# Value rows of a causal attention: unpadded through memory, spread into the padded tile on GpSimd

## The reference

```
xn = layernorm(x)
Q, K, V = (xn @ W.T) split into 16 heads of 16, for W_q, W_k, W_v
scores = Q K^T * 16**-0.5, masked with the lower triangle
s = (softmax(scores) @ V) joined @ W_o.T
```

## Time and profile before

| what | us |
| --- | --- |
| three runs | 2177.48, 2183.09, 2172.04 |
| median | 2177.48 |
| profiled execution, device time | 2176.68 |
| profiled execution, span of the trace | 2174.9 |
| projection, to the first work of the next phase | 0 to 135.5 |
| first product of the causal attention | 137.4 |
| last product of the causal attention | 681 |

### The profile page before, as it was taken

One profiled execution on the slowest core, in us unless ns is written; L12 is line 12 of the kernel. 1 busy time (PEld: TensorE's weight loads), 2 busy tenths in 40 slices (PEclk: granted clock), 3 DMA queues, 4 the chain that ended last, 5 costly groups with the idle time before them and its releaser, 6 DMA issues. The chain is left out here.

```text
span 2174.9 us, 43531 instructions
## 1 busy us (share of the span) xinstructions
PE 1953.3 (90%) x13728; PEld 1388.4 (64%) x13728; DVE 1583.2 (73%) x2778; ACT 1168.5 (54%) x2437; POOL 904.7 (42%) x789
## 2 busy tenths in 40 slices
PE   5869999999996799999996999779999999699976
PEld 4633433343342688888875778668888888578865
DVE  5657778787881699999995554269999999655424
ACT  3415656565665566666664433256666666444323
POOL 3431212112112666666661433276666666243320
PEclk9868999999998899999997999889999999799988
DMA  6892564564532000000022011200000002212137
GB/s 207 274 200 31 72 85 69 71 88 59 76 50 64 13 24 24 24 21 23 22 66 63 30 58 49 96 8 24 24 24 24 24 24 66 60 32 58 49 112 241
DMA packets 164992, 143.13 MB, mean 66 GB/s; under 512 B 31298, under 2 KB 145406, under 8 KB 164734
## 3 DMA queue, kind: packets, MB, share of 16 engines
q1 hardware_dynamic: 163518, 140.14, 27.4%
q10 hardware_dynamic: 1344, 1.31, 0.2%
HBM read 90.80 MB, written 50.35 MB: 65 GB/s over the span
## 5 line engine op out<-in xcount | busy, mean ns | idle before, releaser
L654 DVE TENSOR_REDUCE ca_mx<-ca_pR 128x1 f32<-128x512 f32 (+3 forms) x768 | 376.1, 550 | 90.5 <-PE ca_pR L524 47.7
L631 ACT ACTIVATE ca_pr<-ca_pS 128x1024 f32<-128x1024 f32 (+3 forms) x384 | 300.5, 813 | 242.8 <-PE ca_pS L548 184.2
L888 ACT ACTIVATE w_pe<-w_pS,w_nmax 128x256 f32<-128x256 f32 x512 | 234.4, 484 | 142.0 <-DVE w_nmax L998 142.0
L463 POOL TENSOR_SCALAR_AFFINE_SELECT ca_pr<-ca_pr 128x256 f32<-128x256 f32 x256 | 103.9, 406 | 429.3 <-ACT ca_pr L631 427.0
L811 POOL TENSOR_TENSOR w_tsn<-w_qk,w_tab 128x512 f32<-128x512 f32 x128 | 202.8, 1605 | 176.9 <-DVE w_pn L1007 161.2
L521 PE MATMUL ca_pR<-ca_ks,ca_qs 96*128 96x512 bf16 (+3 forms) x768 | 240.6, 350 | 19.0 <-DVEq L707 16.3
L1007 DVE TENSOR_SCALAR w_pn<-w_pe,w_rsum 128x256 f32<-128x256 f32 x512 | 227.3, 505 | 4.5
L548 PE MATMUL ca_pS<-ca_qs,ca_ks 98*128 98x512 bf16 (+3 forms) x768 | 191.5, 333 | 14.9 <-issue 13.0
L521 PEld LDWEIGHTS ca_pR<-ca_ks,ca_qs 96*128 96x128 bf16 x768 | 73.3, 98 | 186.8 <-DVE ca_mx L654 125.7
L819 POOL TENSOR_TENSOR w_rs<-w_ssc,mhalf 128x16 f32<-128x16 f32 x64 | 187.5, 2929 | 5.3
L1100 PE MATMUL w_pX<-ident,w_pn 128*128 128x128 f32 x1024 | 145.2, 287 | 22.7 <-DVE w_pn L1007 22.2
(11 more groups left out here) (164 smaller groups left out, 4532.8 us busy)
## 6 DMA issues: line engine op xcount, KB each, us to landing
QKP<-p_parts SPq DMA_DIRECT2D x32, 384.0 KB, 3.3
ca_qs<-QKP SPq DMA_DIRECT2D x96, 128.0 KB, 6.6
ca_ks<-QKP SPq DMA_DIRECT2D x96, 128.0 KB, 7.1
VA<-p_vaug SPq DMA_DIRECT2D x8, 1024.0 KB, 5.4
ca_va<-VA SPq DMA_DIRECT2D x16, 512.0 KB, 10.5
w_xt<-X SPq DMA_DIRECT2D x64, 128.0 KB, 2.0
X<-w_x SPq DMA_DIRECT2D x64, 128.0 KB, 1.7
f_hh<-X SPq DMA_DIRECT2D x32, 256.0 KB, 5.0
```

Source lines behind the costliest of these rows:

```text
L631: act.activation(pr[:, k % 2, pair, :, 0:w], pS[:, pair, :, 0:w], ACT.Exp, scale=CS).then_inc(p_ready, 1)
L654: dve.tensor_reduce(mx[:, i, h, ch:ch + 1], pR[jb % RING][:, 0:w], AX.X, ALU.max, negate=True).then_inc(ring_free, 1)
L888: ins = act.activation(pe_[:, h], pS[:, bank, slot], ACT.Exp, bias=nmax[:, n:n + 1], accum_out=sums[:, h:h + 1])
```

## The change

The tensor `VA` holds, for each sequence, group of four heads and partition, the 8 tiles of 64 value floats side by side, without ones and zeros. The projection's staging tile `p1_vst` has the same order, so that a super is stored as 4 groups x 4 tiles x 64 floats for each partition (runs of 256 floats in memory) and holds half the bytes. A group's values are loaded into a new tile `ca_vin`, one run of 512 floats for each partition. In the causal phase POOL sets the zeros and ones of `ca_va` once and copies `ca_vin` into its value columns: slot 0 at the start, then group n + 1 in group n, ahead of the cut of step 2. TensorE waits for both before the first `weighted` of a group.

```
-    va_t = VA.rearrange("(b t p) (g c) -> b g p t c", b=BATCH, p=P, g=CG)
-    return out + [(va[:, u], va_t[n // CG, n % CG])]
+    return out + [(vin[:, u], VA[n // CG, n % CG])]
...
-        vaug = sb("p1_vaug", [P, 2, SUP, CH, VW], F32)
+        vst = sb("p1_vst", [P, 2, CG, SUP, GH * CD], F32)
...
-        va_t = VA.rearrange("(s n p) c -> s p n c", n=SUP, p=P)
+        va_t = VA.rearrange("b g p (f n) c -> b f p g n c", f=2)
...
-                sp.dma_start(va_t[s], vaug[:, j].rearrange("p n h w -> p n (h w)")).then_inc(v_stored[j], 16)
+                sp.dma_start(va_t[it, j], vst[:, j]).then_inc(v_stored[j], 16)
...
-                pool.memset(vaug[:, :, :, :, CD + 1:VW], 0.0).then_inc(v_preset, 1)
-                pool.memset(vaug[:, :, :, :, CD:CD + 1], 1.0).then_inc(v_preset, 1)
...
-                dve.wait_ge(v_preset, ONE + 2)
...
-                    dve.tensor_copy(vaug[:, j, 2 * v:2 * v + 2, :, 0:CD],
-                                    pV[:, v].rearrange("p n (h w) -> p n h w", w=CD)).then_inc(v_copied, 1)
+                    dve.tensor_copy(vst[:, j, :, 2 * v:2 * v + 2],
+                                    pV[:, v].rearrange("p n (g c) -> p g n c", g=CG)).then_inc(v_copied, 1)
...
+            heads = va[:, :, :, :].rearrange("p u t (h w) -> p (u t h) w", w=VW)
+            pool.memset(heads[:, :, CD + 1:VW], 0.0).then_inc(va_preset, 1)
+            pool.memset(heads[:, :, CD:CD + 1], 1.0).then_inc(va_preset, 1)
+
+            def spread(u, it):
+
+                pool.wait_ge(loaded[u % SLOTS], ONE + (it + 1 + u // SLOTS) * LOADS * 16)
+                pool.sem_inc(K.passed, 1)
+                pool.tensor_copy(va[:, u % SLOTS].rearrange("p t (h w) -> p t h w", w=VW)[:, :, :, 0:CD],
+                                 vin[:, u % SLOTS].rearrange("p t (h d) -> p t h d", d=CD)).then_inc(va_ready, 1)
+
+            spread(0, 0)
...
+                    if i == SPREAD_AT and more:
+                        spread(u + 1, it)
...
+                if k == 0:
+                    pe.wait_ge(va_preset, ONE + 2)
+                    pe.wait_ge(va_ready, ONE + n + 1)
...
+        VA = nc.dram_tensor("VA", [BATCH, CG, P, TPB, GH * CD], F32, kind="Internal").ap()
```

More of the change, by code:

```diff
@@ L70, in stack_transfers @@
 def stack_transfers(K, QKP, VA, n, u):
-    qs, ks, va, _ = K.stacks
+    qs, ks, vin, _, _ = K.stacks
     parts = QKP[n].rearrange("(z h d) c s -> z c d h s", z=2, h=GH)
@@ L120, in phase_project @@
         part_stored = [sem(f"p1_part_stored{i}") for i in range(CG)]
-        v_ready, v_copied, v_preset = sem("p1_v_ready"), sem("p1_v_copied"), sem("p1_v_preset")
+        v_ready, v_copied = sem("p1_v_ready"), sem("p1_v_copied")
         v_stored = [sem(f"p1_v_stored{i}") for i in range(2)]
         x_t = x.rearrange("(s n p) d -> s p n d", n=SUP, p=P)
-        va_t = VA.rearrange("(s n p) c -> s p n c", n=SUP, p=P)
+        va_t = VA.rearrange("b g p (f n) c -> b f p g n c", f=2)
         block = c.enter_context(nc.Block())
@@ L163, in rest_of @@
                         for transfer in stack_transfers(K, QKP, VA, 0, 0)[g * share:(g + 1) * share]:
-                            sp.dma_start(*transfer).then_inc(K.stacks[3][0], 16)
+                            sp.dma_start(*transfer).then_inc(K.stacks[4][0], 16)
                 sp.wait_ge(v_copied, ONE + 2 + s * 2 + 2)
-                sp.dma_start(va_t[s], vaug[:, j].rearrange("p n h w -> p n (h w)")).then_inc(v_stored[j], 16)
+                sp.dma_start(va_t[it, j], vst[:, j]).then_inc(v_stored[j], 16)
             def step(s, j, it, final):
@@ L249, in _ @@
         def _(dve):
-            start_at_one(dve, mine + K.stacks[3])
+            start_at_one(dve, mine + K.stacks[4])
             dve.sem_inc(rest_ready, CG)
@@ L360, in phase_causal @@
     LATE_STEP = 1
+    SPREAD_AT = 2
     RJ = NJ + 3
@@ L404, in sem @@
             return mine[-1]
-        qs, ks, va, loaded = K.stacks
+        qs, ks, vin, va, loaded = K.stacks
         mask_q = sb("ca_mask_q", [P, P], BF16)
@@ L424, in phase_causal @@
         s_ready, p_ready, pv_done = sem("ca_s_ready"), sem("ca_p_ready"), sem("ca_pv_done")
-        cut = sem("ca_cut")
+        cut, va_preset, va_ready = sem("ca_cut"), sem("ca_va_preset"), sem("ca_va_ready")
         ot_copied, rec_done = sem("ca_ot_copied"), sem("ca_rec_done")
@@ L1762, in program @@
         QKP = nc.dram_tensor("QKP", [BATCH * CG, P, 3, SEQ], BF16, kind="Internal").ap()
-        VA = nc.dram_tensor("VA", [TOK, CH * VW], F32, kind="Internal").ap()
+        VA = nc.dram_tensor("VA", [BATCH, CG, P, TPB, GH * CD], F32, kind="Internal").ap()
         AO = nc.dram_tensor("AO", [TOK, D], F32, kind="Internal").ap()
@@ L1814, in program @@
                         c1.enter_context(nc.sbuf_tensor("ca_ks", [SROWS, SLOTS, GH, SEQ], BF16)),
+                        c1.enter_context(nc.sbuf_tensor("ca_vin", [P, SLOTS, TPB, GH * CD], F32)),
                         c1.enter_context(nc.sbuf_tensor("ca_va", [P, SLOTS, TPB, GH * VW], F32)),
```

## The result

| | us | ratio to before, 95% interval |
| --- | --- | --- |
| before, median of 20 runs | 2174.27 | |
| after, median of 20 runs | 2170.78 | 0.9984 (0.9976 to 0.9991) |
| forecast | 2173.0 (2163 to 2184) | |

The changed kernel is 3.5 us faster (2.0 to 5.2 by the interval), the forecast was 4.4 us. The first three runs of before had a higher median (2177.48) than the twenty.

What follows compares the result with a forecast made beforehand. The prediction took attention as bound by TensorE's queue and the projection's end by a DMA backlog. Terms -5.0 + 0.2 + 0.4 = -4.4 us against 2176.68 gave 2172.3, forecast as 2173.0 us for the runs' median, range 2163 to 2184.

Steps and rivals of the forecast that it cites:

- The tail: End of the projection, DMA engines full: smaller stores of values and group 0's smaller load save 5.0 us.
- the last store's landing: End of the projection: the last half-size store of values lands in an estimated 3.2 us, against 5.4 for full size.
- The memsets at the start: Start of the projection: removing POOL memsets of 1.7 and 0.3 us gains 0, as POOL then waits anyway.
- The two waits on TensorE: Before the first `weighted` of each of 16 groups: two fulfilled waits cost 0.4 us in all (0 to 2.2).
- The two increments: Before TensorE starts attention: DVE increments two more semaphores, costing 0.2 us.
- The spread: POOL's copy of `ca_vin` into `ca_va`, 15 times in the groups: 0.63 us each, hidden up to 2.8 us, cost 0.
- the memsets of 1.3 and 0.26 us: Start of attention: new POOL memsets of 1.3 and 0.3 us, hidden in POOL's wait, cover left 22 us.
- Nothing of it: Rival, projection's end: the last chain and its landing set the end, so time stays about 2177.5 us; chance 0.17.
- The whole projection paced by DMA: Rival, projection: supers 0 to 4 each gain 1.9 us too, giving about 2163.6 us; chance 0.11.
- The held cut: Rival, step 2 of groups: a 4.0 us copy delays POOL's cut and TensorE, giving about 2191 us; chance 0.10.

Runs made afterwards that it cites:

- experiment 2: The kernel before with its two POOL memsets of the padded staging tile moved ahead of the first reciprocal deviation; 2172.0 us, 0.9987 of before.
- the second series: The changed kernel run once more, unchanged; 2171.24 us, 0.9978 of before.
- experiment 3: The changed kernel with a second store of the same tile behind each store of values, to a tensor nobody reads; 2175.4 us, 1.0003 of before.
- experiment 4: The changed kernel with a POOL memset ahead of each spread in the groups: 2304 elements, 2171.57 us, 0.9969 of before; 4608 elements, 2193.11 us, 1.0074.
- the runs with 2304 elements: The changed kernel with a POOL memset of 2304 elements a partition ahead of each spread in the groups; 2171.57 us, 0.9969 of before.

## Why the prediction was right, and where it was not

**The tail: the mechanism right, its size too large.** Forecast -5.0 us, of which two parts: the last issue 1.34 us earlier, because ACT's wait of 2.86 us shrinks by as much, and 3.7 us at the landing behind it. From the first store of the tail to the first product the six runs whose projection is that of the change took 32.1, 33.4, 33.4, 32.1, 32.5 and 33.6 us, 32.8 in the mean, against 36.5 and 36.4 in the two with the old stores: -3.6 us. This stretch holds the two new increments too (+0.2 us, below), so the tail itself gave -3.8. It splits at the last issue. From there to the first product it is 7.4 to 7.6 us in all six against 10.57 in both old ones, -3.1 us or -3.3 without the increments, where the forecast had -3.7. From the first store to the last issue it is 25.4 us in the mean (24.5 to 26.2) against 25.9, -0.5 us, where the forecast had -1.34. The step that did not come out is this second one. ACT's wait was 1.78 us in after, but ACT's waits for `QKP` stores in super 7 sum to 2.9 to 4.1 us in the other five, and to 2.9 and 4.3 us in the two with the old stores: no shrinking is to be told from their scatter.

The prediction's estimate of 3.2 us for the last store's landing rests on a fit that the Trainium skill (DMA: Bandwidth & Descriptors, Anatomy of one DMA) gives for DMAs issued by GpSimd. The half-size stores of this kernel, issued by SP, land after 3.5 us in the median.

**The memsets at the start: costed at 0, worth -1.5 us.** The step "where POOL then waits anyway" looked at POOL alone. DVE's first xn ran beside the memset and was held by it (experiment 2). The trace of before had the sign of it: these four instructions took 2.89 us once, and 2.1 to 2.2 in later supers. The Trainium skill (SBUF — State Buffer, Who interferes with whom) names the mechanism: copies and `tensor_scalar` of DVE can enter a mode that needs the port pair shared with GpSimd, and whoever comes second waits for the whole instruction. The prediction used this rule for the added POOL work and not for the removed one. The trace agrees for the memset: 2.89 against 1.38 us, with the first of the four ending 0.4 us behind the memset. For POOL's operation in the later supers the hold was shorter than that rule gives (last section).

**The two waits on TensorE: taken at +0.4 us, measured at 0.** The lower bound held: equal gaps with and without them. **The two increments: +0.2 us** stands: from SP's first issue of attention to TensorE's first product 1.87 us before, 2.05 after. **The spread: 0**, at 0.61 us where 0.63 was taken, and the memsets of 1.3 and 0.26 us as taken, with a cover of 22.6 us left behind them.

**The sum** by measured terms is -3.8 - 1.5 + 0.2 = -5.1 us, just within the interval of -5.2 to -2.0 (the second series has -6.7 to -2.6). The first products agree: 132.6 in the mean of six against 137.4, 4.8 us. That the sum lies so near the forecast of -4.4 is partly luck: a tail taken 1.2 too large, a missed 1.5 and 0.4 for waits that cost nothing. The first product, forecast at 132.4, was hit by the same luck. One slip is in the range: by the prediction's own bounds (-2 for the tail, +0.2, +2.2 for the waits) it reaches up to +0.4 us, not -0.5.

**The rivals.** Nothing of it: excluded by the interval and by experiment 3. The whole projection paced by DMA: supers 1 to 5 are as far apart in after (98.72 - 45.56 = 53.2 us) as before (100.89 - 47.02 = 53.9), and 54.5 us in the repetition. The held cut: experiment 4.

## What to carry to other kernels

Bytes count where a backlog ends a phase, so look for the window in which the DMA engines are full and ask what else is in it: moving the loads out of that window brought the first product 3 us forward, about as much as halving the stores did, and by the runs 3 to 7 us. When an instruction is removed from one engine, look at what the other engines did beside it: a GpSimd instruction that nobody is waiting for can still hold up DVE. On TensorE two waits a group that were surely fulfilled cost nothing here, and sixteen more cost 0.8 us.

## What was not expected of the hardware

The four `tensor_scalar` of DVE took 1.38 us alone, 2.2 us beside a GpSimd operation of 1.15 us, and 2.89 us beside a memset of 1.70 us, which only writes. The two differ in one point: beside the memset the first of the four is held to the memset's end and then takes its 0.4 us. Beside the other operation, in after at 34.56 us, it takes 1.24 us and ends at 35.80, only 0.15 us behind that operation's end, so by this row it was not held for the whole of it (spans on POOL are rough).

Part of this kernel's scatter sits in the loop of its attention. Every third group, where the loop of three groups turns, the gap between late stores is 34.9 to 37.5 us instead of 31.1 or 31.4, and differs from one execution to the next (35.7, 36.3, 34.9 in after; 36.2, 36.3, 36.8 in its repetition), while nearly all other gaps agree to 0.03 us. From first to last product the attention took 539.9 to 545.9 us in the kernels of this study without longer groups. It is not the only place: the time behind the last product varied from 1490 to 1496 us. TensorE stands still at the turn with nothing that the list of waits shows, in after:

```profile
PE ca_pS L559 <- issue: 9.6, 3, 3.6
```

and at most of these halts the granted clock falls from 2.4 to 1.2 GHz. Where it did not fall, the gap is 34.9 us (once in before, once in after); where it fell for 3.4 us, 35.7 to 37.1; for 6.8 us, 36.7 to 37.5. In the halt from 296.3 to 299.7 in before it fell near 298.7; in after TensorE stood from 288.8 to 291.8, and it fell only near 292.9. What TensorE stood still for was not tried. The DMA queues hold a candidate: in each of the 15 halts of five profiles (before, after, its repetition, and the runs with 2304 elements and without the two waits) one of the packets of 0.02 MB moved that the profile calls instruction (queue q8), of which a stretch of 10 us otherwise has mostly one or none. So TensorE may wait for its own code there; no run shows that.
